# One transformer layer on one core: each pair of scores a word of the plan, the norms applied in halves

## What is computed

```
h = token_table[x] + segm_table[mask] + pos
q, k, v = split(layernorm(h) @ w_qkv.T)       # 12 heads of 16
q = layernorm(q) * 16 ** -0.5;  k = layernorm(k)
h = h + (softmax(q @ k.T) @ v) @ w_proj.T
xq  = round(clip(layernorm(h) / a1, -8, 7))
g   = gelu(xq @ wq1.T * alpha_w1 * a1 + b1)   # 768 wide
h = h + round(clip(g / a2, -8, 7)) @ wq2.T * alpha_w2 * a2 + b2
```

## Time and profile before

| | us |
|---|---|
| median of 3 runs | 1070.74 |
| lowest and highest | 1069.35, 1071.54 |
| span of the profiled execution, first to last instruction | 1067.6 |
| TensorE, ScalarE, VectorE, GpSimd busy | 979.4, 872.6, 813.9, 411.8 |

### The profile page before, as it was taken

How to read it: one execution, slowest core, us unless ns; L and a number is a source line. 1 busy time by engine, 2 the same in 40 slices (tenths; PEclk the granted TensorE clock), 3 DMA queues, 4 the chain that set the end, 5 groups by cost and what they waited for, 6 DMA issues and landing times.

```text
span 1067.6 us, 19577 instructions
## 1 busy us (share of the span) xinstructions
PE 979.4 (92%) x7571; PEld 389.1 (36%) x7571; DVE 813.9 (76%) x2325; ACT 872.6 (82%) x950; POOL 411.8 (39%) x345
## 2 busy tenths in 40 slices
PE   5589999999999999999999999999999999989885
PEld 4333433334342433434343343434334343413223
DVE  5878869788686969878696977869697886825347
ACT  1387788897979889797988979798888989798883
POOL 6555513635343353534435363443526412201000
PEclk9899999999999999999999999999999999999997
DMA  7511200303011040202102040110202000000000
GB/s 162 127 16 16 31 1 2 46 1 64 12 25 22 1 75 1 38 8 58 18 2 45 1 73 3 31 16 16 30 1 45 1 16 1 16 1 1 16 1 31
DMA packets 25762, 28.62 MB, mean 27 GB/s; under 512 B 5027, under 2 KB 22182, under 8 KB 25670
## 3 DMA queue, kind: packets, MB, share of 16 engines
q0 software_dynamic: 16896, 11.80, 9.4%
q1 hardware_dynamic: 8624, 15.55, 4.8%
q10 hardware_dynamic: 150, 0.01, 0.0%
HBM read 21.06 MB, written 6.29 MB: 26 GB/s over the span
## 4 chain that ended last, share of the span: by engine, by line
PE 40%; ACT 30%; DVE 24%; issue 3%; POOL 3%; DMA 0%
ACT probs L682 22%; PE ps_o L1247 12%; PE ps_s L1227 8%; PE ps_j L1271 4%; ACT gelu L676 4%; PE ps_j L1279 3%; PE ps_j L1325 3%; POOL stack L592 3%; PE ps_j L1286 2%; PE ps_j L1292 2%; ACT L676 2%; ACT L682 2%; DVE hn L797 2%; PE ps_j L1311 2%; PE ps_j L1296 2%
## 5 line engine op out<-in xcount | busy, mean ns | idle before, releaser
L682 ACT ACTIVATE probs<-ps_s 128x1024 f32<-128x1024 f32 x768 | 736.1, 1023 | 125.5 <-PE ps_s L1227 120.6
L1247 PE MATMUL ps_o<-probs,v_sb 128*32 128x512 f32 x3072 | 394.7, 605 | 0.2 <-DVE o_sb L859 0.2
L1227 PE MATMUL ps_s<-qT,kT 64*128 64x512 f16 x1536 | 264.3, 384 | 35.0 <-ACT probs L682 25.2
L592 POOL TENSOR_TENSOR stack<-sq,stack 128x384 f16<-128x384 f32 x124 | 120.5, 992 | 162.9 <-DVE stack L846 162.9
L1227 PEld LDWEIGHTS ps_s<-qT,kT 64*128 64x128 f16 x1536 | 61.5, 93 | 299.5 <-ACT probs L682 267.6
L525 POOL DMA_INDIRECT h_all<-in_L_tok_token_table,idx x60 | 96.7, 1611 | 59.5 <-DMA h_all<-in_L_tok_segm_table,idx 41.2
L1247 PEld LDWEIGHTS ps_o<-probs,v_sb 128*32 128x32 f32 x3072 | 69.1, 109 | 124.3 <-issue 116.1
L601 POOL TENSOR_TENSOR y_sb<-y_sb,b_row 128x768 f32<-128x768 f32 x14 | 25.4, 1814 | 198.8 <-DVE y_sb L931 198.8
L581 POOL TENSOR_TENSOR sq<-qk 128x384 f32<-128x384 f32 x56 | 46.2, 826 | 139.5 <-DVE qk L894 139.5
L525 POOL DMA_INDIRECT h_all<-in_L_tok_segm_table,idx x56 | 87.2, 1557 | 15.2 <-issue 13.1
L1279 PE MATMUL ps_j<-wh,partsT 128*128 128x384 f16 (+1 forms) x384 | 71.5, 296 | 1.0 <-ACT partsT L663 0.7
(11 more groups left out here) (201 smaller groups left out, 1118.5 us busy)
## 6 DMA issues: line engine op xcount, KB each, us to landing
out<-h_all SPq DMA_DIRECT2D x15, 384.0 KB
h_all<-in_positions SPq DMA_DIRECT2D x7, 768.0 KB
gelu<-in_L_ffn_w SPq DMA_DIRECT2D x2, 576.0 KB
h_all<-in_L_tok_token_table,idx POOLq DMA_INDIRECT x60
h_all<-in_L_tok_segm_table,idx POOLq DMA_INDIRECT x56
probs<-in_L_attn_qkv_weight SPq DMA_DIRECT2D x2, 432.0 KB, 4.7
h_all<-in_positions SPq DMA_DIRECT2D x2, 384.0 KB, 8.0
o_nat<-in_L_ffn_alpha_a SPq DMA_DIRECT2D x1, 384.0 KB
```

The source lines that it names most:

```text
L592: last = nc.gpsimd.tensor_tensor(low, src, high, ALU.subtract)
L682: nc.scalar.activation(probs[:, u % PROBS, 2 * pair:2 * pair + 2], ps_s[:, 2 * pair:2 * pair + 2], ACT.Exp, scale=SCORE_SCALE).then_inc(ex ...
L1227: last = mm(ps_s[:, j], kT[rows, par, head // 2, m * P:(m + 1) * P], qT[rows, par, head // 2, nh * NQ:(nh + 1) * NQ], start=True, stop=True)
L1247: last = mm(ps_o[32 * j:32 * j + 2 * D, :], v_sb[:, par, m, (GH * group + j) * VE:(GH * group + j) * VE + 2 * D], probs[:, u % PROBS, j], ...
```

## The change

`PLAN` gets the word s: one pair of scores, with its exp on ScalarE. All engines walk one flat list of words, and GpSimd too: q is a square, L a low part, a the addition of Y, p and t the gathers of segments and tokens. The order of TensorE's, VectorE's and GpSimd's words is new. N and m are written twice, each for two tiles. The first pairs' waits on D and E stay with the first pair. The n of a tile waits for job D of the tile two before it as well as for E. In halfstep 0 and before, s s stands at the head of each line, and GpSimd's words at the end of the last, with N for all four tiles. In the diff the same splitting of `square`, `split_low` and `second_norm` is left out, and the walks of VectorE and TensorE.

```diff
 PLAN = """
-h h o
-Y0 Y1 Y2 F0 Y3 F1
-G0 F2 F3 H0 G1 P0
-h h
-G2 G3 W0 W1 W2 H1 H2 H3
-h l0 h R0
-W3 m0 h
-W4 h
-h N0 W5 I0
-I1 h o A0
-I2 h A1 A2
-h A3 I3
-C0 B0 X0
-X1 B1 r0 X2 X3 B2 X4 X5 r1 B3 h r2 h r3 g h
-h
-h S0 n0
-h n1 o
-D0 x0 E0 C1
-n2 h C2 D1
-E1 n3 h
-D2 h x1
-h D3 E2 x2
-E3 x3 x4 h
-x5 C3 h
+s o h h s
+s Y0 F0 F1 s F2
+s G0 F3 s G1 H0 G2 P0
+s q0 s h h
+s s G3 H1 H2 H3 W0
+s s h h W1
+s s h p0
+s l0 h R0 s q1 h W2
+s N0 m0 s h A0 Y1 o W3
+s s A1 B0
+s m1 q2 Y2 r0 s B1 W4
+s h s W5
+s h N1 s I0 Y3 A2
+s q3 I1 I2 s I3 A3 C0 C1 B2 r1 g X0 r2 X1 B3 x0 X2 X3 h r3 S0 a0 X4 L0 X5
+s s h n0 h h C2 n1
+s L1 C3 x1 s h L2 o
+s s L3 h n2
+s D0 x2 s E0 D1 n3 t0
+s h s
+s h s h
+s E1 x3 s D2 E2
+s h s
+s h s D3 E3 x4 x5
+s h s
...
-S0.1 n0.1 C1.1 C2.1
-h
-h
-h n1.1 D0.1 E0.1 n2.1
...
-w1.2 h D3.2 E3.2
+s s S0.1 n0.1 C1.1 C2.1
+s s h
+s s h
+s s h n1.1 D0.1 E0.1 n2.1
...
+s s w1.2 h D3.2 E3.2 q0.2 q1.2 q2.2 q3.2 L0.2 L1.2 L2.2 L3.2
...
-    return {"X": t % 2, "B": 2}[kind] if kind in "XB" else IN_TURN.index(job) % BANKS
+    return {"X": t % 2, "B": 2, "W": t % BANKS}[kind] if kind in "XBW" else IN_TURN.index(job) % BANKS
...
             def one(s0, s, b):
-                add_result(s0, s)
                 ahead = s0 + GATHER_AHEAD
-                if FIRST_GATHERED <= ahead < HALVES:
-                    add_segments(ahead)
-                    add_tokens(ahead)
-                square(s0, s)
-                split_low(s0, s)
+                for kind, t, at in step_work(s0):
+                    if kind == "a":
+                        add_result(s0, s)
+                    elif kind == "p" and FIRST_GATHERED <= ahead < HALVES:
+                        add_segments(ahead)
+                    elif kind == "t" and FIRST_GATHERED <= ahead < HALVES:
+                        add_tokens(ahead)
+                    elif kind == "q":
+                        square(s0, s, t)
+                    elif kind == "L":
+                        split_low(s0, s, t)
...
-                    if u == GELU_UNIT and job_runs("X", s0):
+                for kind, t, at in step_work(s0):
+                    if kind == "g" and job_runs("X", s0):
                         for j in range(HB):
                             gelu_out(s0, s, j)
-                    for pair in range(2):
-                        if attends(s0):
-                            exps(s0, s, u, pair)
+                    elif kind == "s" and attends(s0):
+                        exps(s0, s, t // 2, t % 2)
...
+                here = slice(0, TH) if s0 <= 0 else slice(2 * i, 2 * i + 2)
+                for t in range(TH)[here]:
                     last = ts(hn[:, t], h_tile(half, t), mv[:, 0, t, 0:1], rn[:, 0, t:t + 1],
                               ALU.subtract, ALU.mult)
                 link(last)
-                link(nc.vector.tensor_copy(parts[:, :, 0:C], hn[:]))
-                tt(parts[:, :, C:2 * C], hn[:], parts[:, :, 0:C], ALU.subtract).then_inc(hn_ready, 1)
+                link(nc.vector.tensor_copy(parts[:, here, 0:C], hn[:, here]))
+                tt(parts[:, here, C:2 * C], hn[:, here], parts[:, here, 0:C], ALU.subtract).then_inc(hn_ready, 1)
...
+                    dve.wait_ge(job_mm["D"], half * TH + (t - 1))
                     dve.wait_ge(job_mm["E"], half * TH + (t - 1))
...
-                for j in range(GH):
-                    if j % 2 == 0 and (u or attends(s0 - 1)):
-                        pe.wait_ge(exp_done, 2 * UNITS * s + (2 * u - 1 + j // 2))
+                if u or attends(s0 - 1):
+                    pe.wait_ge(exp_done, 2 * UNITS * s + (2 * u - 1 + pair))
+                for j in (2 * pair, 2 * pair + 1):
                     head = GH * group + j
                     rows = slice(head % 2 * (P // 2), (head % 2 + 1) * (P // 2))
                     last = mm(ps_s[:, j], kT[rows, par, head // 2, m * P:(m + 1) * P],
                               qT[rows, par, head // 2, nh * NQ:(nh + 1) * NQ], start=True, stop=True)
-                    if j % 2:
-                        last.then_inc(scores_mm, 1)
+                last.then_inc(scores_mm, 1)
...
+                    elif s0 >= 1:
+                        pe.wait_ge(hn_ready, 2 * (half - 2) + t // 2 + 1)
...
-                    if t == 0:
-                        pe.wait_ge(xq_ready, nth(half, 0, 1))
+                    pe.wait_ge(xq_ready, 2 * half + t // 2 + 1)
...
+                    if kind == "s" and attends(s0):
+                        scores(s0, s, t // 2, t % 2)
```

More of the change, by code:

```diff
@@ L570, in _, with square @@
             gather(tok_table, 0, 1, tok_added[1])
-            def square(s0, s):
+            def square(s0, s, t):
                 if not job_runs("B", s0):
@@ L575, in square, with split_low @@
                 half = job_half("B", s)
[L576 to L583, removed]
+                pool.wait_ge(job_out["B"], nth(half, t, TH))
+                if job_half("B", s0) > 2 or t >= 2:
+                    pool.wait_ge(summed, half * TH + (t - 1))
+                nc.gpsimd.tensor_tensor(sq[:, t % 2], qk[:, t], qk[:, t], ALU.mult).then_inc(squared, 1)
+            def split_low(s0, s, t):
                 if not job_runs("D", s0):
                     return
[L586 to L593, removed]
+                pool.wait_ge(high_ready, nth(job_half("D", s), t, TH))
+                parts_ = list(stack_parts(t))
+                for high, low, src in parts_ if s0 > -2 else parts_[:1]:
+                    last = nc.gpsimd.tensor_tensor(low, src, high, ALU.subtract)
+                last.then_inc(stack_ready, 1)
             def add_result(s0, s):
@@ L620, in _ @@
             add_segments(3)
-            split_low(-2, -2)
+            for t in range(TH):
+                split_low(-2, -2, t)
             add_tokens(2)
-            split_low(-1, -1)
+            for t in range(TH):
+                split_low(-1, -1, t)
             add_tokens(3)
@@ L864, in head_outputs, with second_norm @@
                 ins.then_inc(heads_out, 1)
-            def second_norm(s0, s):
+            def second_norm(s0, s, i):
                 half = job_half("I", s)
-                link(ts(ra2[:], rn[:, 1], ia1[:], None, ALU.mult))
-                for t in range(TH):
+                if i == 0:
+                    link(ts(ra2[:], rn[:, 1], ia1[:], None, ALU.mult))
+                here = slice(2 * i, 2 * i + 2)
+                for t in range(TH)[here]:
                     last = ts(xf[:, t], h_tile(half, t), mv[:, 1, t, 0:1], ra2[:, t:t + 1],
@@ L1047, in one @@
             def one(s0, s):
[L1048 to L1052, removed]
-                                head_outputs(s0 - 1, s - 1, passes(s0 - 1) - 1)
-                            if t and attends(s0):
-                                head_outputs(s0, s, t - 1)
-                        elif at is None:
-                            work(s0, s, kind, t)
-                        else:
-                            work(at, at, kind, t)
+                for kind, t, at in step_work(s0):
+                    if kind == "o":
+                        if t == 0 and attends(s0 - 1):
+                            head_outputs(s0 - 1, s - 1, passes(s0 - 1) - 1)
+                        if t and attends(s0):
+                            head_outputs(s0, s, t - 1)
+                    elif at is None:
+                        work(s0, s, kind, t)
+                    elif kind not in "sh":
+                        work(at, at, kind, t)
             def step(ins):
@@ L1328, in one @@
             def one(s0, s, b):
[L1329 to L1339 removed]
+                for kind, t, at in step_work(s0):
+                    if kind == "s" and attends(s0):
+                        scores(s0, s, t // 2, t % 2)
+                    elif kind in job_mm:
+                        job(s0 if at is None else at, s if at is None else at, kind, t)
+                    elif kind == "h" and t >= HEADS_BEHIND and attends(s0):
+                        heads(s0, s, t - HEADS_BEHIND)
+                    elif kind == "h" and t < HEADS_BEHIND and attends(s0 - 1):
+                        heads(s0 - 1, s - 1, UNITS + t - HEADS_BEHIND)
             def tail():
```

89 lines of the change are left out of this document (37 added, 52 removed).

## The result

The changed kernel takes **1098.97 us** (median of 4 runs, 1097.87 to 1099.89) against 1071.14 us for the kernel before in the same comparison: ratio 1.0266, 95% interval 1.0251 to 1.0280. It is slower by 2.7%, where 1040 us and a gain of 30.5 us were forecast, and it lies outside the range.

A forecast was written before the change was run, and what follows sets the result against it. TensorE and ScalarE both stand near the bound but lose time to each other. 57.0 + 0.9 + 0.55 + 1.0 = 59.5 us a halfstep against 61.6; with the ends 30.5 us less, 1040 us, range 1016 to 1066.

The forecast's parts named there:

- the walk of the plan: New order priced job by job, pair by pair: TensorE the fuller engine; a period above 61 us would disprove it.
- 59.5 us: Forecast steady halfstep, summed from TensorE's work and waits: 2.1 us less than the 61.6 before.
- The halves of the norms: VectorE's norms written as two halves: some 0.5 us more work, hidden; A0 should not wait, at most 1.4 us.
- 57.0 + 0.55: TensorE's work in a steady halfstep, 57.0 us, plus 0.55 us for score runs rising from 24 to 35.
- The 0.9 for pairs: TensorE's waits for exps before pairs: some five of 0.1 to 0.2 us, 0.9 us a halfstep.
- the 1.0 for the gelu: TensorE's waiting around line 14's gelu, which starts up to 1 us late: 1.0 us, bounds 0 and 2.
- the part on GpSimd's queue: GpSimd's new order, with a0 between q3 and L0: S0 slowed by half of 3.6 us, swallowed by slack.
- just hidden: L0 done at 43.4 to 45.5 us of the halfstep, D0 wanted at about 45.4: no loss counted.
- rival 3: Slower: all of a0 (3.6 us) falls on S0 and delays GpSimd's queue; halfstep 62.7, 1080 us; chance 0.11.
- The rule of the Trainium skill: Two-SBUF-input VectorE instructions and GpSimd instructions reading SBUF exclude each other for their whole length; would give 1059 us.
- nearly every step: By the exclusion rule, nearly every step of VectorE's S0 would wait for a0's two operations.
- The ends: Half of the first period's 2.1 us, then 1.5 and 2.8 us from the last two; nothing after the last gelu.

The follow-up runs named there:

- the small a0: The changed kernel with GpSimd's addition of Y (a0, two operations) cut to 8 columns each, waits and signals kept: 1052.73 us, ratio 0.9838.

## Why the prediction was wrong

**What held.** The total of the walk of the plan. The changed kernel's period is above 61, which was to disprove the walk; but its 59.5 us is met by the first period (59.57) and by the steady ones with the small a0 (59.59), so what pushed the period up was not in TensorE's order. That TensorE is the fuller engine, that the pairs wait little, and that pairs apart are a gain (22 us where compared alone) is right. The halves of the norms cost A0 nothing in the steady state, as said.

The terms of that sum agree less well than their total. In the row of the small a0 above TensorE is busy 58.35 us, where 57.0 + 0.55 was forecast. It waits 1.19: 0.75 at D1 and 0.44 for a copy of ps_o, neither of them in the sum. The 0.9 for pairs and the 1.0 for the gelu show as no wait of TensorE's between 340 and 880 us. The work was 0.8 us too low and the waits 0.7 too high, and that the two cancel is luck.

**The step that failed** is in the part on GpSimd's queue: "In the new order a0's 3.6 us lie right beside it: bounds 0 and 3.6 us later. I take half, which the slack swallows." Three things were wrong in it.
- The place. a0 was put at 35.8 to 39.5 us of the halfstep, ahead of S0. It meets x0 first, which stands ahead of r3 and so of S0; x0 was not in the sum at all. The price, 1.50 + 1.05 = 2.55 us, is itself inside the bounds of 0 and 3.6.
- The slack. D0 was called "just hidden" with L0 done at 43.4 to 45.5 and D0 wanted at 45.4, and D1 "closer still". A first period that already has D1 waiting 0.75 without a0 shows that there was none; 2.49 of the 2.55 reached D0 and D1.
- The clock. No term stood for it. The stalls of 3.24 us were followed by 6.8 us at 1.2 GHz, which made another 2.4 in the halfstep shown, and by half of that time in every third one. With it a halfstep averages 63.72, not the 62.7 of rival 3, which named the queue and was given 0.11. Its stall of 3.2 us is right to the tenth, but by luck: it put all 3.6 us of a0 onto S0, and the runs show 2.5 us, half of them by way of x0, on top of a wait of 0.75 that was there without a0.

The rule of the Trainium skill that was weighed there ("SBUF — State Buffer", Who interferes with whom) spoke for the loss, and was set aside for "half". It was the rule for VectorE instructions with two SBUF inputs. The two that a0 held are tensor_scalars with one input, to which the other rule of that section applies, the one named with the result. And it was not "nearly every step": in the changed kernel a0 holds one tensor_scalar per operation of its own, no more, since each held one ends with it.

**The gelu.** 1.0 us was put on a late start, to be hidden if the table load did not wait with it. That is what came: the load runs while X0 is still awaited, directly behind the exp before it, and the block from load to load takes 6.44 us (405.58 to 412.02), 0.3 more than in the kernel before (6.15 from 396.51). One correction to the description of the kernel before: its gelu comes ahead of the exps of unit 13, counted from 0 (26 exps into the halfstep), not of unit 12; the changed plan has 28 ahead of it.

**The ends.** The first stretch was expected to bring half a period (about 1 us). It brought a loss: the first gelu load comes 4.6 us later; 1.94 of it is the gelu's new place, two exps further on, which is no loss of time by itself, and the rest falls in halfstep 1, where the halves and W are. The period before the last gained its 1.5 us only without a0 (59.11 us there). For the last, 2.8 us were forecast: it takes 58.22 against 58.34, and the last gelu block is 7.70 us long (1036.85 to 1044.55; 6.14 in the kernel before). In spans, the kernel with the small a0 gains 23.65 in twelve periods, 1.49 in the next and 0.22 in the tail, and loses 0.24 in the last and 9.62 in the first stretch, of which 2.6 lie before the first exp, in code that the change leaves alone: 15.5 us of the forecast's 30.5. This first stretch is not a firm number. The changed kernel runs the same work there, with its first exp 0.9 us earlier than in the kernel before, and reaches the first gelu 5.0 us sooner than the kernel with the small a0. The ends are the second step that was mis-sized: without a0's cost the time is 1052.73, still 13 us above the forecast.

## What to carry to other kernels

Work on a half-idle engine has a price at the place where it lies: look up which of VectorE's operations stand beside GpSimd's, one by one, and how far each is from the engine that bounds. A slack of tenths of a us at the end of a chain of five handovers is no slack; take the upper bound there. And if a stall of 2 to 3 us would come back in each round, look for a row that shows what TensorE's clock does after such a stall before a price is put on it. Last, a sum that comes out right is not yet a set of right terms: compare each with the rows.

## What the runs showed of the hardware

- A VectorE tensor_scalar of only 96 columns took 1.88 us instead of 0.21 beside a GpSimd addition of 1.83 us: it ended at 418.16, the addition at 418.08. A tensor_reduce of 384 columns beside the same kind of addition kept its 0.54.
- Stalls of 1.97 and 1.27 us, with 1.3 us of work between them, in a stream that is otherwise full, were followed by about 6.8 us at 1.2 GHz in one period and 3.4 us in the next (a granted clock of 0.72 and 0.86 over 12 us). In the kernel with a0 behind L3, stalls of 0.76, 0.43 and 1.36 us were not followed by any (clock 1.00 from 410 to 440 us).
- A gelu's table load starts right behind the exp ahead of it (403.62 + 1.94, then the load at 405.58), so it hides a wait for its input.
